# Stores of finished tiles handed from the engine that adds to the queue that loads, four parts for each tile

## What is computed

```python
w = weight[adapter_ids]                       # 8 adapters of 512x512, one for each batch element
c = einsum('bsi,boi->bso', x, w)
dense = c @ ffn_weight.T + bias
out = where(query_sel[:, None] & row_sel[None, :], dense, 0)
x = x + out
```

## Time and profile before

| | us |
|---|---|
| median of 3 runs (lowest, highest) | 633.07 (631.84, 633.16) |
| the profiled execution | 633.0 |
| its span, first to last instruction | 631.3 |
| PE busy | 562.3 (89%) |
| DVE busy | 423.3 (67%) |
| POOL busy | 367.9 (58%) |
| ACT busy | 182.5 (29%) |

### The profile page before, as it was taken

One profiled execution on the slowest core, in us unless ns is written; L12 is line 12 of the kernel. 1 busy time (PEld: TensorE's weight loads), 2 busy tenths in 40 slices (PEclk: granted clock), 3 DMA queues, 4 the chain that ended last, 5 costly groups with the idle time before them and its releaser, 6 DMA issues.

```text
span 631.3 us, 10738 instructions
## 1 busy us (share of the span) xinstructions
PE 562.3 (89%) x3298; PEld 470.9 (75%) x3298; DVE 423.3 (67%) x877; ACT 182.5 (29%) x346; POOL 367.9 (58%) x385
## 2 busy tenths in 40 slices
PE   0899999999999998869999988998899999899780
PEld 0689999999999853646667766787788886678570
DVE  6797667657756784655768755795456668688680
ACT  4443333322222213323333423342221132111110
POOL 5422264765665573464667766976596100688885
PEclk9899999999999999889999999998899999999995
DMA  6977567689887226894677898998896630466631
GB/s 193 204 215 219 157 147 224 169 234 241 247 235 216 85 78 201 258 298 165 228 242 259 266 362 293 357 363 296 295 348 242 200 104 15 146 220 214 238 143 58
DMA packets 91239, 136.87 MB, mean 217 GB/s; under 512 B 29048, under 2 KB 45790, under 8 KB 90162
## 3 DMA queue, kind: packets, MB, share of 16 engines
q1 hardware_dynamic: 75314, 95.08, 51.3%
q0 software_dynamic: 12912, 40.45, 16.5%
q10 hardware_dynamic: 2960, 0.67, 0.6%
HBM read 87.17 MB, written 50.84 MB: 219 GB/s over the span
## 4 chain that ended last, share of the span: by engine, by line
PE 55%; POOL 13%; DMA 12%; DVE 8%; issue 5%; SPq 4%; ACT 1%; POOLq 0%; ACTq 0%; DVEq 0%
PE acc L2076 16%; PE work L2020 9%; PE acc L2302 9%; POOL out_tile L1053 5%; POOL out_dram L1044 5%; PE bcast L2173 3%; DMA x_by_tile<-x_rows 3%; PE bcast L2291 3%; DMA two_rows<-expert_deltas_sorted 2%; PE work L2004 2%; PE work L2243 2%; PE bcast L2134 2%; DMA cond_w<-in_L_cond_weight_dram 2%; PE acc L2207 2%; PE acc L2173 2%
## 5 line engine op out<-in xcount | busy, mean ns | idle before, releaser
L948 POOL TENSOR_TENSOR yT_lo<-y_masked,yT_hi 128x512 fp32r<-128x512 f32 x29 | 38.3, 1322 | 72.7 <-ACT yT_hi L1122 72.6
L1253 ACT ACTIVATE x1T_hi<-work 128x512 fp32r<-128x512 f32 x66 | 39.4, 598 | 139.5 <-PE work L2243 139.0
L985 POOL DMA_INDIRECT gated_by_expert<-records,record_places x64 | 62.8, 981 | 20.2 <-issue 17.2
L1771 DVE TENSOR_TENSOR x1T_lo<-work,x1T_hi 128x512 fp32r<-128x512 f32 x66 | 45.3, 686 | 43.1 <-PE acc L2302 22.0
L1732 DVE TENSOR_TENSOR x_group<-acc,base_b_bc 128x512 f32<-128x512 f32 x79 | 50.3, 682 | 23.4 <-PE acc L2209 23.4
L2020 PE MATMUL work<-uT_hi,hankel 128*128 128x512 f32 (+3 forms) x256 | 64.8, 326 | 0.8 <-DVE y_masked L1505 0.8
L2302 PE MATMUL acc<-merged_w_hi,x1T_hi 128*128 (+1 forms) x156 | 46.0, 417 | 5.4 <-DVE x1T_lo L1771 5.4
L1025 POOL DMA_INDIRECT expert_deltas_sorted<-x_group,two_rows x36 | 35.9, 997 | 22.8 <-DVE x_group L1732 15.8
L2020 PEld LDWEIGHTS work<-uT_hi,hankel 128*128 128x128 f32 x256 | 45.7, 189 | 3.8 <-issue 1.0
L1053 POOL TENSOR_TENSOR out_tile<-out_tile,cond_w 128x512 f32<-128x512 f32 x14 | 18.2, 1301 | 48.9 <-DVE out_tile L1921 48.6
L1025 POOL DMA_INDIRECT expert_deltas_sorted<-x_group,records_of_slots x31 | 30.5, 985 | 26.3 <-DVE x_group L1732 19.0
(11 more groups left out here) (367 smaller groups left out, 1351.2 us busy)
## 6 DMA issues: line engine op xcount, KB each, us to landing
hankel<-k_rev SPq DMA_DIRECT2D x32, 512.0 KB, 6.9
x_group<-in_x_dram SPq DMA_DIRECT2D x32, 256.0 KB, 3.8
cond_w<-in_L_cond_weight_dram SPq DMA_DIRECT2D x28, 256.0 KB, 4.3
x_rows<-x_base_sorted SPq DMA_DIRECT2D x25, 256.0 KB, 5.0
x_by_tile<-x_rows SPq DMA_DIRECT2D x25, 256.0 KB, 4.6
x_rows<-x_by_tile SPq DMA_DIRECT2D x24, 256.0 KB, 3.0
two_rows<-expert_deltas_sorted SPq DMA_DIRECT2D x10, 512.0 KB, 5.6
cond_w<-expert_deltas_sorted SPq DMA_DIRECT2D x9, 512.0 KB, 6.0
```

Source lines behind the costliest of these rows:

```text
L948: g.tensor_tensor(yT[h % 2][1][:, :, :], y32[h % 2][:, :, :], yT[h % 2][0][:, :, :].bitcast(F32), ALU.subtract).then_inc(y_lo, 1)
L985: g.indirect_dma_start(rec_dram, bass.IndirectOffsetOnAxis(ap=place_u[to][:, m:m + 1], axis=0), both[:, m, :], None, bounds_check=last_pla ...
L1253: a.activation(xts[n % 2][0][:, :, :], wb[n % 2][:, :], ACT.Copy).then_inc(xd_hi, 1)
L1771: v.tensor_tensor(xts[n % 2][1][:, :, :], wb[n % 2][:, :].rearrange("p (k b) -> p k b", k=LB), xts[n % 2][0][:, :, :].bitcast(F32), ALU.su ...
```

## The change

Kept tiles 0 to 8 (`IN_PARTS = 9`) are stored by SP. As the indirect store by a table belongs to GpSimd, SP stores a kept tile as four parts of 32 rows, one batch element each, at an address that it reads from a new table `elem_of` (the batch element at each of the 4 places of tiles 16 to 31) into a register. Kept tiles 9, 10 and 11 stay with POOL.

```diff
+        def element_of(eng, t, q):
+            return eng.value_load(elem_of[0:1, q, t - GROW:t - GROW + 1], min_val=0, max_val=B - 1)
+
+        def store_part(eng, k, q, element):
+            eng.dma_start(out[bass.ds(element, 1), :, :].rearrange("o h l -> (o h) l"),
+                          kept[k][H * q:H * q + H, :]).then_inc(s_dr[0], 16)
@@ the turns at which kept tiles are finished by DVE
-            n = j - CHOSEN - 2 * LAG
-            return 0 if j <= CHOSEN else (j - CHOSEN + 1) // 2 if n <= 0 else min(KEPT, LAG + 2 * (n // 3) + min(n % 3, 2))
+            n = j - CHOSEN - 8
+            return 0 if j <= CHOSEN else (j - CHOSEN + 1) // 2 if n <= 0 else 4 + n if 4 + n <= IN_PARTS else min(
+                KEPT, IN_PARTS + (4 + n - IN_PARTS) // 2)
@@ SP, in each turn of the tail
                 for k in range(kept_out_by(j - 1), kept_out_by(j)):
+                    elements = [element_of(sp, KEPT_TILES[k], q) for q in range(TB)] if k < IN_PARTS else []
                     if k + 2 < KEPT:
                         sp.wait_ge(k_rdy, k + 1)
                         load_rows(KEPT_TILES[k + 2], rows_kept[k % 2], s_rk[k % 2])
+                    for q, element in enumerate(elements):
+                        store_part(sp, k, q, element)
@@ POOL, finish(i) and the turns
+                if SWEPT[i] == NX:
+                    pool.wait_ge(s_dr[0], parts_stored(IN_PARTS))
                 store_out(SWEPT[i], outt[n][:, :], s_out[n])
...
-                for k in range(kept_out_by(j - 1), kept_out_by(j)):
+                for k in range(max(IN_PARTS, kept_out_by(j - 1)), kept_out_by(j)):
                     pool.wait_ge(k_rdy, k + 1)
                     store_out(KEPT_TILES[k], kept[k][:, :], s_kout)
@@ the table, at some 60 us: DVE, PE, DVE
+                v.tensor_scalar(here, slot_v[:, :, GROW:NX], place[:, 0:1], None, ALU.is_equal).then_inc(t_mat, 1)
...
+                for q in range(TB):
+                    last = mm(bb[0][0:1, 128 + (NX - GROW) * q:128 + (NX - GROW) * (q + 1)], quad[:, q, q, 0:1],
+                              here[:, q, :], start=True, stop=True)
...
+                v.tensor_scalar(elem_of[:, :, :], bb[0][0:1, 128:128 + TB * (NX - GROW)]
+                                .rearrange("p (q t) -> p q t", q=TB), -1.0, None, ALU.add).then_inc(t_rdy, 1)
```

## The result

The changed kernel takes 640.55 us (median of five runs, 635.29 to 642.52), the one before 631.79 us beside it (median of six, 628.35 to 633.16). The ratio is 1.0155, 95% interval 1.0114 to 1.0196: **1.5% slower**, 9.8 us by the ratio and 8.8 by the medians. (A sixth run of the changed kernel, 667.09 us with TensorE's clock at 0.829 of full speed over the whole span instead of 0.961 to 0.967, is disturbed and left out; with it the median is 641.13.) The profiled execution took 640.55 us. The forecast was 631.9 us, in a range of 627.8 to 636.0.

What follows compares the result with a forecast made beforehand. POOL's backlog was taken to bound the kernel. From the profiled 633.0 us, the last store 2.5 us earlier, 1.0 us for gaps and 0.4 for the table gave −1.1 us: 631.9 us, range 627.8 to 636.0.

Steps and rivals of the forecast that it cites:

- What bounds the kernel: Tail: POOL, never let go again once started, is a backlog; at most 9 us before PE and DVE bound.
- The sum is made against the profiled execution: Whole kernel: the forecast starts from the profiled 633.0 us and adds the change's terms to it.
- PE is late by 1.4 from there on.: First kept step: SP's parts delay swept tile 9's row load by 1.5 us, making PE 1.4 late.
- Swept tiles 4 to 12. 8 × 2.60 later: POOL in the tail: tile 12 is added 8 × 2.60 us after tile 4, at 574.7 against 577.06.
- A turn of SP ... 5.35 us.: Kept tiles 4 to 8, turns 13 to 17: SP takes 5.35 us, bounds 4.8 and 6.2, where PE needs 3.22.
- The end changes by 5 us for each us of SP's turn: Tail: five such turns lie ahead of the wait; 4.8 us gives 629.1, 6.2 us gives 636.1.
- The new wait: POOL's store of swept tile 20 could go at 603 but waits for kept tile 8's parts, landing at 605.5.
- rival C: Parts land 4.6 us after issue, sharing the queue with row loads: 1.5 us more, 633.4 us; chance 0.10.
- 18.2 us: POOL behind the wait: six finishes and the stores of kept tiles 10 and 11, up to the last store.
- 1.0 of POOL's gaps: Tail: 1.0 us added for POOL's gaps, of the 1.2 us before that could not be assigned.
- The table at 60 us: Around 61 us: four more products on PE for the table cost 0.4 us, taken in full.
- rival B: SP's turn from 5.8 us on makes the kernel slower, over 634.3 us, 636.1 with 6.2; chance 0.22.

Runs made afterwards that it cites:

- the second trace: The changed kernel run and profiled once more, nothing changed: 1.0151, 638.99 us against 630.06 for the kernel before.
- Run 9: kernel 7 with SP's four register loads of kept tile 0 moved ahead of its first wait of the tail: 0.9998 of the kernel before.
- run 11: The changed kernel with SP storing only kept tiles 0 to 3, POOL the others, no extra stores: 1.0043 of the kernel before.
- experiment 2: The changed kernel without the parts' register loads, its 36 parts going to fixed places of another buffer: 0.996 of the kernel before.
- experiment 3: The changed kernel with two of each kept tile's four parts, and their register loads, given to ScalarE's queue: 0.9947 of the kernel before, 627.17 us.
- kernel 7: The changed kernel with nine extra small indirect stores by POOL in its idle time before the tail, 39 DMAs: 1.0043 of the kernel before, 635.46 us.
- 6: The kernel of experiment 3 with five extra small indirect stores by POOL in idle time before the tail, 35 DMAs: 0.9902 of the kernel before, 624.03 us.
- 12: The kernel of experiment 3 with five extra POOL stores and SP's two register loads of kept tile 0 read ahead: 0.9895 of the kernel before, 622.54 us.
- experiment 1: The kernel before with only the new turns for finishing kept tiles, POOL still storing all of them: 1.0005 of the kernel before.

## Why the prediction was wrong, point by point

**What bounds the kernel** was read rightly: a backlog of POOL that starts once and ends last. The nine stores took 9.0 us of busy time from it.

**The step that failed most** is the first: "The sum is made against the profiled execution", with the last store's time as the only thing that moves. The 5.1 us behind it were taken as a constant. They hold POOL's drain, which is 5.06 us with 39 DMAs and 10.29 with 30. This is 5.2 us, beside 4.8 of the tail, and the prediction had no term, rival or bound for it. Nothing in the single trace of before could have given its size, but the row on the drain stood there, starting at 626.0 and ending with the kernel while the last store had landed by 629.0, and was worth a rival.

**"PE is late by 1.4 from there on."** Mis-sized. SP's own part was right: the row load goes 6.90 us after the first add, where 6.7 was worked out. But the load landed after 4.5 us (4.2 in the second trace) instead of 2.57, behind four parts on the same queue; I had assumed no change there. Why it landed later isn't shown (see the last section). With it PE is 2.0 us later than forecast, beside SP's 0.2. Then PE, after its wait, worked at the lower clock: from taking the rows to DVE's bias behind the matmuls it was 5.04 us (548.55 to 553.59), and had been some 3.4 before (547.74 to 551.1, the masks of the earlier trace rows less 0.7). That is 1.7 more than forecast, and the three make the 3.95 by which the add of tile 4 is later than forecast. Run 9 took only the register loads of this step away and got 2.7 us of the tail back; run 11 showed that the step by itself outweighs the four stores' 5.2 us, since POOL stands idle through two of them.

**"Swept tiles 4 to 12. 8 × 2.60 later"**: right, 20.8 us (555.03 to 575.83).

**"A turn of SP ... 5.35 us."** Mechanism right, shown by runs 2 and 3; size too low. Turns were 5.6 to 5.8 us in the second trace and 5.8 to 7.1 in the first. The parts (0.52 apart) were as priced, the kept row load took 0.55 instead of 0.45. The four register loads took 2.9 to 3.0 us in the first trace and 2.7 in the second, not 2.5. I chose 0.62 for one between 0.54 and 0.80; 0.68 to 0.75 was right, since in the turns that matter each batch of four had one slow load (0.85 to 1.02 us, 0.50 to 0.85 in the second trace). The Trainium skill ("DMA: Bandwidth & Descriptors", "Latency and other measured facts") states a floor of about 600 ns for one. By that the prediction came to an estimated turn of 5.9 us, without its working; 0.60 with the 0.17 of the two register instructions, four times, beside 2.83 for the rest gives it. The trace has 0.27 us for most loads, so there is no such floor here, and yet that turn was a little nearer than mine.

**"The end changes by 5 us for each us of SP's turn"** was too steep. The chain shows turn 14 still released by POOL's add of tile 14 (582.84), and SP unbroken only from there: the rest of that turn and three more. 0.95 us more per turn gave 2.9 us (68.39 − 49.49 = 18.9 us over three turns, against 16.0), not 4.7.

**The new wait** was right in place and kind. POOL went on 2.5 us after the last part's issue (3.1 taken; the part had landed after 1.75), so rival C didn't come about; it ended late, at 610.14, since all ahead of it was late. **18.2 us** behind it were 18.07. DVE's waits for kept rows in turns 15, 16 and 17 came too, at 1.8, 3.6 and 2.4 us, where some 3 each was named. PE's last tile was to be 4 us later than before and is much later: it starts at 618.58, 81.5 us after the first add, where it was 70.9 before and 74.9 by the forecast. That cost nothing: DVE was done with it by 623, and POOL, held up by the wait, came to it at 626.66.

**"1.0 of POOL's gaps"**: too much. The gaps stand at fixed counts of DMAs: those of 0.62 ahead of the 4th and 0.76 ahead of the 13th (0.28 ordinarily) are there before and after; the 1.35 ahead of the 35th fell away, and with it went the short drain. Behind the wait no gap is over 0.30; only that ahead of the 13th, 0.48 more than ordinary, lies ahead of tile 14's add, from which SP's chain starts.

**The table at 60 us** (0.4 us) was not tested by itself. On average the first add starts no later in the 14 traces with the table (534.2 to 541.5, mean 537.2) than in the three without (536.7 to 540.5, mean 539.0), so nothing speaks for a cost.

**The sum once more**, against 631.9: tail 7.3 longer than forecast (91.11 − 83.8), drain 5.2 longer, 1.4 of it already given to gaps and table, and a tail that began 2.8 earlier in this trace: 631.9 + 7.3 + 5.2 − 1.4 − 2.8 = 640.2, of 640.55 measured. Without the long drain the changed kernel would stand where kernel 7 does, 1.0043 or 634.5 us: where **rival B** (a turn over 5.8 us) put it, but more than half of the lateness came from the first step. The 2.8 us of the earlier start are chance, and make this trace look better than the change is.

What stays open: why the drain falls at the 35th DMA. Only the dependence on the count is shown, at 30, 31, 34, 35, 39 and 48, and the gap ahead of the 35th suggests that the same work is done either there or at the end, though it is 1.1 us longer than an ordinary one and the drain 5.6 us shorter. How much the lower clock costs by itself was not isolated: it also fell in traces of faster kernels (3, 6 and 12) and, at 585 us, in that of experiment 1, whose time is that of before.

## What to carry to other kernels

Before work is moved from one queue to another, price the whole of what the receiving queue then does per turn, and look at what waits behind it: 1.30 us of a backlogged engine was exchanged for 4.9 us of a queue on which three other engines' rows depend, and the same parts on two queues turned a loss of 1.5% into a gain of 0.5%. Read the instructions behind the last piece of work, too: a drain at the end belongs to the time, and here it depended on how many DMAs had been issued. A small first delay in a pipelined tail can be more than its own length: here the four register loads ahead of one row load cost POOL 4 us (experiment 9), with the later landing and PE's slower restart behind them.

## What the runs showed of the hardware

POOL's last drain, by the number of its indirect DMAs from the 48 us of idle time on:

| DMAs | 30 | 31 | 34 | 35 | 39 | 48 |
|---|---|---|---|---|---|---|
| drain, us | 10.29 | 10.29 | 10.54 | 4.73 | 5.07 | 5.80 |

It grows by some 0.08 us for each DMA past the 35th, and repeats to within 0.01 us between kernels with the same count (10292 ns in five traces with 30 or 31). Five small stores more in idle time, which nothing reads, shorten the drain by 5.6 us and bring the gap of 1.35 back, 4.5 us net by the traces; between kernels 3 and 6 the measured gain is 0.45 points, 2.8 us (each ratio is good to some 0.35 points).

A register load by SP takes 0.27 us and now and then 0.4 to 1.0 (in 6 of the 36 of the changed kernel's first trace); start to start 0.55 with the two register instructions behind it. The batches of four in SP's long turns took 2.7 to 3.0 us.

Row loads of 256 KB that are issued right behind small stores landed later: the one for tile 9 took 4.5 and 4.2 us behind four parts in the changed kernel's two traces, 4.5 in experiment 11 and 3.3 in experiment 2, and 3.6 behind two parts in experiment 3, against 2.57 before. Whether the shared queue or the traffic does it isn't shown: in experiment 3, with half of the parts on another queue, the medians of the tail (3.6, 3.7, 4.4) are no shorter than here. The DMA issues of the tail, after (size, median us to landing):

```profile
x_rows<-x_by_tile SPq DMA_DIRECT2D x14, 256.0 KB, 2.9
cond_w<-x_by_tile SPq DMA_DIRECT2D x10, 256.0 KB, 3.7
out_dram<-dense_kept SPq DMA_DIRECT2D x36, 64.0 KB, 2.7
two_rows<-x_by_tile SPq DMA_DIRECT2D x5, 256.0 KB, 4.0
```

Before, the loads into `cond_w` and `two_rows` both had 2.6 in the same stretch; those into `x_rows` had 3.1, so they did not get slower.
